# Two decoder layers on one core: later shift transposes, a wider order of the side work, a spread-out start, and GpSimd adding the two key halves of the exponentials

## What is computed

```python
x = layernorm(x + linear_attention(x))                     # "L0_attn", buckets of 64
x = layernorm(x + xattn(x, ctx))                           # two attentions, below
x = layernorm(x + moe(x, 16 experts, top 4, gelu))         # every expert on every token
x = layernorm(x + causal_attention(x, 16 heads of 64))
x = layernorm(x + cross_attention(x, ctx, 16 heads of 8))
x = layernorm(x + moe(x, 8 experts, top 2, capacity 40, relu))

def mha(x, y, ..., causal):                                # twice in xattn: on itself, then on ctx
    q, k, v = ln(x) @ wq, ln(y) @ wk, ln(y) @ wv           # 16 heads of 32
    a = softmax(q @ k.T * 32 ** -0.5)
    if causal: a = a * keep_earlier_keys                   # after the softmax: all keys stay in the sum
    x = x + a @ v @ li1 + b1
    return x + gelu(ln(x) @ li2 + b2) @ li3 + b3
```

## Time and profile before

| | |
|---|---|
| median of 3 runs (lowest to highest) | 918.81 us (918.29 to 922.25) |
| the profiled execution's own time | 918.41 us |
| its span, first to last instruction | 916.6 us |
| busy: PE, DVE, ACT, POOL | 776.5, 490.6, 433.4, 194.0 us |
| mean granted TensorE clock | 0.91 of full |

### The profile page before, as it was taken

One profiled execution on the slowest core, in us unless ns is written; L12 is line 12 of the kernel. 1 busy time (PEld: TensorE's weight loads), 2 busy tenths in 40 slices (PEclk: granted clock), 3 DMA queues, 4 the chain that ended last, 5 costly groups with the idle time before them and its releaser, 6 DMA issues.

```text
span 916.6 us, 16466 instructions
## 1 busy us (share of the span) xinstructions
PE 776.5 (85%) x6048; PEld 564.3 (62%) x6048; DVE 490.6 (54%) x1345; ACT 433.4 (47%) x1079; POOL 194.0 (21%) x272
## 2 busy tenths in 40 slices
PE   3675888887879798899999998989888888989866
PEld 1344666655655565568989896867665454757555
DVE  3675684746455565624454336544455666564542
ACT  1121556445454545474454447656553554434301
POOL 1111453434321211111000005432331010101100
PEclk9855998979798997999999999999999798989989
DMA  9206651514233443400000000000001400000000
GB/s 272 79 4 136 141 129 42 114 45 97 55 89 100 111 106 81 142 1 1 1 1 1 1 1 2 2 1 1 1 2 47 139 2 2 2 8 2 6 6 8
DMA packets 20496, 45.34 MB, mean 49 GB/s; under 512 B 5721, under 2 KB 9385, under 8 KB 20417
## 3 DMA queue, kind: packets, MB, share of 16 engines
q1 hardware_dynamic: 18688, 40.83, 17.6%
q10 hardware_dynamic: 1728, 3.45, 1.2%
HBM read 17.89 MB, written 0.52 MB: 20 GB/s over the span
## 4 chain that ended last, share of the span: by engine, by line
PE 67%; DVE 13%; ACT 9%; issue 7%; DMA 2%; SPq 2%; ACTq 0%; POOL 0%; POOLq 0%; DVEq 0%
PE G L502 10%; PE SC L681 7%; PE SC L743 6%; PE SC L730 6%; PE SM L692 5%; PE SO L715 5%; PE G L544 4%; PE G L507 3%; ACT causal_probs L1061 3%; PE SC L657 3%; PE G L842 2%; PE SO L797 2%; PE SC L765 2%; PE SM L664 2%; DVE negmax L1442 2%
## 5 line engine op out<-in xcount | busy, mean ns | idle before, releaser
L1076 ACT ACTIVATE exps<-SC 128x512 f32<-128x512 f32 x192 | 113.2, 599 | 144.4 <-PE SC L681 143.7
L1434 DVE TENSOR_REDUCE shift_cols<-SC 128x2 f32<-128x512 f32 x192 | 130.6, 687 | 62.0 <-PE SC L657 61.5
L1511 POOL TENSOR_TENSOR rstd<-variance,consts 128x2 f32<-128x2 f32 x52 | 37.0, 712 | 317.9 <-DVE variance L1136 317.9
L1577 POOL TENSOR_TENSOR unit_sums<-unit_sums,unit_inverse 128x256 f32<-128x256 f32 x48 | 35.5, 740 | 261.3 <-ACT unit_inverse L1082 261.3
L1050 ACT ACTIVATE hidden<-SC,cols 128x256 f32<-128x256 f32 x128 | 53.6, 471 | 68.5 <-PE SC L730 68.4
L1061 ACT ACTIVATE causal_probs<-SC,negmax 128x128 f32<-128x128 f32 (+1 forms) x128 | 52.3, 424 | 40.8 <-DVE negmax L1442 40.6
L681 PE MATMUL SC<-stacked_q,stacked_k 100*128 100x256 f32 x256 | 69.0, 355 | 1.7 <-DMA stacked_q<-shift_rows 0.8
L743 PEld LDWEIGHTS SC<-ffn_w,hidden 128*128 128x128 f32 x512 | 66.9, 194 | 5.3 <-issue 2.0
L1587 POOL TENSOR_TENSOR causal_probs<-causal_probs,inverse 128x256 f32<-128x256 f32 x64 | 51.6, 828 | 81.3 <-DVE inverse L1447 81.3
L1468 DVE SCALAR_TENSOR_TENSOR R<-SC,small,R 128x128 f32<-128x128 f32 x128 | 39.0, 346 | 55.4 <-PE SC L743 55.0
L743 PE MATMUL SC<-ffn_w,hidden 128*128 128x128 f32 x512 | 68.5, 278 | 0.0
(11 more groups left out here) (259 smaller groups left out, 1532.3 us busy)
## 6 DMA issues: line engine op xcount, KB each, us to landing
stacked_k<-k_hi SPq DMA_DIRECT2D x64, 128.0 KB, 2.4
stacked_q<-q_hi SPq DMA_DIRECT2D x64, 128.0 KB, 2.4
ffn_w<-in_ffn_w SPq DMA_DIRECT2D x16, 512.0 KB, 4.5
stacked_k<-k_lo SPq DMA_DIRECT2D x32, 128.0 KB, 2.4
stacked_q<-q_lo SPq DMA_DIRECT2D x32, 128.0 KB, 2.4
rows<-in_rows ACTq DMA_DIRECT2D x1, 840.0 KB, 6.5
a_weights<-in_a_li ACTq DMA_DIRECT2D x3, 256.0 KB, 8.7
w_a_li<-in_a_li SPq DMA_DIRECT2D x3, 256.0 KB, 4.6
```

The lines of the kernel that those rows point to most:

```text
L1076: fn(exps[:, n % EXPS, :, :].rearrange("p t q -> p (t q)"), SC[1][:, n % 2, :, :].rearrange("p t q -> p (t q)"), ACT.Exp, scale=ATTENTIONS ...
L1434: v.tensor_reduce(shift_cols[:, n // UNIT % 4, :, n % UNIT], SC[0][:, n % 2, :, :], axis=AX.X, op=ALU.max, negate=True).then_inc(head_max, 1)
```

## The change

1. TURN_AT goes from 5 to 6: PE's transposes, ACT's copy and SP's shift DMA of a unit come one slot later, three slots ahead of their use and no longer four.
2. The order of the sides: `project` starts at 16s-8 (before 16s-11) and draws its values at steps 14 and 15, which is slots 16s+6 and 16s+7; DVE copies both value tiles, where ACT copied one. `enter`, `route` and `causal_in` move by 1 to 3 slots. SP's stacks lie at steps 2, 4, 6, 9 and 12.
3. Slack: PE's transposes behind a norm, and what follows from them, come one or two slots later than DVE's normalising (in `after`: 4 to 5, 5 to 6, 11 to 13, 17 to 20, 14 to 17; in `mix` the 25 steps become 31; in `settle` and `causal_out` one more slot).
4. Start and loads: `linear` starts at slots -22, -13, -6 and 2; qkv is loaded first; the waits for constants, tables and masks move to where they are used; DVE converts the masks at slot 0; the weights of the later stages are loaded by SP in `after(0)` and not ahead of the first stacks.
5. In A2 and LX POOL adds the two key halves of each head's exponentials into `kept` (128x256), at the slot behind the exponential, and PE's `unit_sum` then takes 4 matmuls in place of 8 and waits for POOL.

```diff
-TURN_AT, SUMS_AT, INVERT_AT, VALUES_AT, REFINE_AT, DIVIDE_AT = 5, 15, 16, 17, 17, 18
+TURN_AT, SUMS_AT, INVERT_AT, VALUES_AT, REFINE_AT, DIVIDE_AT = 6, 15, 16, 17, 17, 18
...
-    return FIRST + (0, 2, 5, 8)[b]
+    return (FIRST, FIRST + 9, FIRST + 16, 2)[b]
...
-    return HEADS * b - 12
+    return HEADS * b - 10
...
-    return HEADS * s - 11
+    return HEADS * s - 8
...
                 def unit_sum(U_):
                     n = UNIT * U_
-                    pe.wait_ge(head_exp, n + UNIT)
                     g = fill(pe, "unit", ("S", U_))
-                    for kt in range(TT):
+                    if stream_of(n) // NB == A1:
+                        pe.wait_ge(head_exp, n + UNIT)
+                        for kt in range(TT):
+                            for k in range(UNIT):
+                                last = mm(g[HD * k:HD * k + HD, 0:T], ones, exps[:, (n + k) % EXPS, kt, :],
+                                          start=kt == 0, stop=kt == TT - 1)
+                    else:
+                        pe.wait_ge(kept_ready, n + UNIT)
                         for k in range(UNIT):
-                            last = mm(g[HD * k:HD * k + HD, 0:T], ones, exps[:, (n + k) % EXPS, kt, :],
-                                      start=kt == 0, stop=kt == TT - 1)
+                            last = mm(g[HD * k:HD * k + HD, 0:T], ones,
+                                      kept[(n + k) % EXPS].rearrange("p t q -> p (t q)"), start=True, stop=True)
...
-                    yield 24
-                    copied(("v", s, 0), values(s, 0, 0, 512), lambda g: g[:, :])
...
+                def add_key_tiles(n):
+                    pool.wait_ge(head_exp, n + 1)
+                    wait_filled(pool, ("O" if stream_of(n - EXPS) // NB == A1 else "S", (n - EXPS) // UNIT))
+                    if n == STACK_HEADS:
+                        wait_filled(pool, ("OC", 4 * NB - 1))
+                    v.tensor_tensor(kept[n % EXPS].rearrange("p t q -> p (t q)"), exps[:, n % EXPS, 0, :],
+                                    exps[:, n % EXPS, 1, :], ALU.add).then_inc(kept_ready, 1)
...
                     if n is not None and stream_of(n) // NB == A1:
                         keep(n)
+                    elif n is not None:
+                        add_key_tiles(n)
...
-                for group in ("ctx", "a2", "m0", "lx", "m1", "l1"):
+                for group in ("ctx", "a2"):
                     load_group(group)
...
-                    yield 3
+                    yield 2
                     stack(s, "k", U_)
                     yield 4
                     stack(s, "q", U_)
-                    for j, step in ((1, 7), (2, 10), (3, 13)):
+                    for j, step in ((1, 6), (2, 9), (3, 12)):
```

More of the change, by code:

```diff
@@ L142, in route_at @@
 def route_at(b):
-    return after_at(NB + b) + 16 if b < 2 else after_at(2 * NB - 1) + 17
+    return after_at(NB + b) + 19 if b < 2 else after_at(2 * NB - 1) + 20
 def settle_at(b):
@@ L150, in causal_in_at @@
 def causal_in_at(b):
-    return settle_at(b) + 4 if b < 2 else L1_AT + PAIRS * (b - 1) + 1
+    return settle_at(b) + 5 if b < 2 else L1_AT + PAIRS * (b - 1) + 1
 def causal_out_at(b):
@@ L1171, in heads, with make_masks, make_choice @@
                     return x.rearrange("p (h d) -> p h d", d=HD0)
-                dve.wait_ge(consts_in, 16)
-                at = CONSTS["ident"][0] + 3 * HD
-                v.tensor_copy(choice, consts[3 * HD:3 * HD + UNIT, at:at + UNIT].unsqueeze(2).to_broadcast([UNIT, UNIT, T]))\
-                    .then_inc(masks_made, 1)
-                dve.wait_ge(mask_parts_in, 16)
-                for k, part in enumerate((pair_of16, later_pair16, first_of16, second_of16)):
-                    v.tensor_copy(part[:, :], mask_parts[:, k * P:(k + 1) * P]).then_inc(masks_made, 1)
-                dve.wait_ge(tables_in, 32)
+                def make_masks():
+                    dve.wait_ge(mask_parts_in, 16)
+                    for k, part in enumerate((pair_of16, later_pair16, first_of16, second_of16)):
+                        v.tensor_copy(part[:, :], mask_parts[:, k * P:(k + 1) * P]).then_inc(masks_made, 1)
+                def make_choice():
+                    dve.wait_ge(consts_in, 16)
+                    at = CONSTS["ident"][0] + 3 * HD
+                    v.tensor_copy(choice, consts[3 * HD:3 * HD + UNIT, at:at + UNIT].unsqueeze(2)
+                                  .to_broadcast([UNIT, UNIT, T])).then_inc(choice_made, 1)
                 def linear(b):
@@ L1250, in project @@
                                 op0=ALU.mult, op1=ALU.subtract).then_inc(*emptied((side, s, m)))
-                    yield 25
-                    g = wait_filled(dve, ("v", s, 1))
-                    v.tensor_copy(values(s, 1, 0, 512), g[:, :]).then_inc(*emptied(("v", s, 1)))
+                    for t in range(TT):
+                        yield 14 + t
+                        g = wait_filled(dve, ("v", s, t))
+                        v.tensor_copy(values(s, t, 0, 512), g[:, :]).then_inc(*emptied(("v", s, t)))
                 def after(s):
@@ L1472, in front @@
                 def front(slot):
+                    if slot == 0:
+                        make_masks()
                     if head_of(slot) is not None:
@@ L1647, in after @@
                 def after(s):
+                    if s == 0:
+                        for group in ("m0", "lx", "m1", "l1"):
+                            load_group(group)
                     if s == NB - 1:
-                        yield 13
+                        yield 15
                         wait_filled(sp, ("li3", s, 1))
```

135 lines of the change are left out of this document (69 added, 66 removed).

## The result

| | before | after |
|---|---|---|
| median of 4 runs (lowest to highest) | 919.03 us (918.29 to 922.25) | 862.21 us (857.17 to 872.49) |
| profiled execution, its span | 918.41, 916.6 us | 867.06, 865.3 us |

The ratio is 0.934, with a 95% interval of 0.926 to 0.942. Ratios leave out executions that are over 1.5% above the fastest of their kernel (here 872.49 us), medians do not. The time forecast was 862.

The account below looks back on a forecast made before the run. PE's program order, with a few late producers in it, was taken to set the time. Attention -44 (-27 - 12 - 8 - 12 + 15), LX -13, start 0: 918.8 - 57 = 862 us; range 835 to 903.

Parts of the forecast that it names:

- Bank and gelu, -27: Attentions: later transposes and moved gelu cut PE's 30.4 us of waits for the shared bank to 3.5, -27 us.
- Slack, -12: Attentions: transposes placed later behind a norm remove 12 of PE's 15.0 us of norm waits.
- Clock, -12: Attentions: 25 of 61 us at 1.2 GHz return to full clock, -12 us; bounds 0 and -26.
- the clock doesn't rise: Rival: no clock gain in the attentions, 874 us; inside the forecast's range, whose chance of 0.60 includes it.
- What comes back, +15: Attentions: removed waits uncover others (score bank ring, ACT's latency, SP's queue), +15 us; bounds 0 and 45.
- 0, and 5 us once: SP's later weight loads beside stream 2's stacks: no cost, or 5 us once if the stacks lack spare slots.
- The rival of the shift row as the bound: Rival: PE waits for shift DMAs at 28 units, deciding from 2 us each; at 2.7 us each 937 us; chance 0.05.
- Adds, -16 and +4: POOL's adds halve unit sums, -8 us in A2 and -8 in LX; longer normalising through the port lock, +4 us.
- the second rival: POOL gives nothing: lock costs 16 us in place of 4, lighter sums lower the clock, 4 us; 878 us, chance 0.08.
- Start, 0: Before slot 16: first scores at 70 us, 8 earlier, but DVE work moves into slots 0 to 11; 0, bounds -10 and +10.
- slot 16 at 100 to 105 us: Last step of the start term: slot 16 reached at 100 to 105 us, against 101.5 before the change.
- LX and the end, -13: Third attention to the end: waits -9, sums -8, port +2, uncovered waits +2, together -13 us.

Follow-up runs that it names:

- e6: The kernel before with TURN_AT = 6 alone: 890.4 us, ratio 0.969.
- e7: The kernel before with the first feed-forward matmul (li2) and its gelu one slot later, no other edit: 902.6 us.
- e8: The kernel before with POOL's adds and the halved unit sums in A2 only: 919.1 us, ratio 1.000.
- e2: The kernel before with POOL's adds and the halved unit sums in both A2 and LX, no other edit: 935.8 us, ratio 1.014.
- e4: The changed kernel with the four linear attentions back at their old start slots (-22, -20, -17, -14): 850.8 us, ratio 0.921.
- e9: The changed kernel with the old start slots and POOL's adds in A2 only: 845.0 us, ratio 0.923.
- e1: The changed kernel without POOL's adds, unit sums of 8 matmuls again in A2 and LX: 875.0 us.
- e3: The changed kernel with TURN_AT back at 5, the gelu staying at its new slot: 861.2 us, ratio 0.932.
- e13: The changed kernel with old start slots, adds in A2 only, TURN_AT 5 in LX and SP's later weight loads seven slots later: 859.9 us, ratio 0.933.

## Why the prediction came out

The mechanism of the attentions was right; that the number came to within a microsecond is luck. The changed kernel's own runs are spread over 15 us, and in the profiles the parts add up to -51.3 us where -57 was forecast: the start cost 10.3 us where 0 was booked, the attentions gave 50.1 and not 44, the last stage 9.9 and not 13, and the middle 1.6 and not 0.

**Bank and gelu, -27: right, and for the reason given, but the shares weren't.** Of 30.0 us of waits for the logarithm none is left, where 3.5 us were kept. I wrote of the gelu's 3.3 us stalls, and these are only half of it, five waits. The other half are short waits, which the later turn removes and the moved gelu doesn't (e6, e7).

**Slack, -12: right.** The norm waits between the marks are 16.9 us before and 5.4 after.

**Clock, -12: right in the attentions and too small there, absent from the whole.** In the attentions the share at 1.2 GHz falls from 22% of 295.4 us to 10% of 245.3, so 40 us return and not 25, worth about 18 us (40 x 0.9 busy / 2). Together with the 8 us of sums that is 26, and the busy time fell by 23.8; the booked terms were 8 + 12. No term was booked for the clock elsewhere, and there the start and the last stage took nearly as much time at 1.2 GHz as the attentions gave back. The rival "the clock doesn't rise" is true of the whole span, and false of the stage that it was meant for.

**What comes back, +15: the size was right.** (Its upper bound of 45 was more than the 39 us that the two wait terms had booked.) The idle time falls by 26.3 us, where the three idle terms gave 27 + 12 - 15 = 24. The largest new wait is a kind that I named, the shift row behind SP's queue, and I had set SP's loads at "0, and 5 us once": it is 5.42 us, once. Timelines of SP (last load, last stack issue before the shift row, and the shift row) and of PE:

```profile
146.06 0.43 SPq L1630 DMA_DIRECT2D w_l_wo<-in_l_wo  x1
...
150.09 1.57 SPq L1654 DMA_DIRECT2D stacked_q<-q_lo  x1
151.70 0.71 SPq L1683 DMA_DIRECT2D stacked_q<-shift_rows  x1
```

```profile
156.16 0.80 PE L680 MATMUL SC<-stacked_q,stacked_k 100*128 100x256 f32 x2 [5.42 <-DMA stacked_q<-shift_rows]
```

The rival of the shift row as the bound fell: 8.4 us in 3 waits, where it needed 2 us at each of 28 units.

**Adds, -16 and +4: the sum holds for A2 in the changed kernel, the argument behind it doesn't.** GpSimd's add, and DVE's normalising in A2, cost what was read from A1:

```profile
L1591 POOL TENSOR_TENSOR VB<-exps x128: 715/727/1256, 236.2 to 810.4; 128x256 f32<-128x256 f32 x128
```

```profile
L1150 DVE TENSOR_SCALAR Z<-R,moments,rstd x8: 334/744/891, 253.5 to 349.1; 128x128 f32<-128x128 f32 x8
```

In LX, for which A1's price was booked too, most of the normalising is as short as without adds (the same line from 650 to 850 us):

```profile
L1150 DVE TENSOR_SCALAR X<-R,moments,rstd x10: 336/341/766, 668.1 to 826.5; 128x128 f32<-128x128 f32 x10
```

TensorE waits for GpSimd for 0.2 us in all. But I priced the adds as if half a microsecond of TensorE in a unit were half a microsecond anywhere. e8 shows that without slack A2's are worth nothing (the second rival's mechanism, in the kernel where nothing covers the longer normalising). e2 shows that in LX of the kernel before less work for TensorE went with a lower clock that cost more than it saved, 17 us net; the prediction had this as 4 us in a rival. In the changed kernel's order LX's adds show neither gain nor loss beyond the noise: e4 against e9 and e1's last stage say so, and e3, which has them, has the shortest last stage of all.

**Start, 0: wrong; it costs 10.3 us, the end of the bound.** The first scores came at 68.7 us (forecast 70), but the first values at 113.6. The step that failed is the last, "slot 16 at 100 to 105 us": I took DVE as nearly busy through slots 0 to 11. Slot 16 came at 112.7 us, behind the 110 us that the prediction named as a sign of being wrong. Windows after:

```profile
40.00:68.60 28.60, 17.48 (x57) 10.74 (x58) 15.70 (x63) 6.99 (x17) 2.83 (x4) 0.62 0.23 51
68.60:113.60 45.00, 31.80 (x130) 22.10 (x129) 31.64 (x96) 11.54 (x27) 9.10 (x14) 0.66 0.29 64
```

From the first scores to the first values DVE is busy for 31.6 of 45 us, 70%. Up to the first values its work is the same in both kernels, 63 us; four chains abreast fitted it into 103 us, one or two at a time need 114.

**LX and the end, -13: -9.9 in the profile.** Waits for the norm and for the router's choice, 16.4 us before, are no longer among the long ones. The two halves of the term are both off: TensorE's idle time fell by 14.6 us, where 9 less 4 was booked, and its busy time rose by 4.7 us, where the sums were to take 8 away, at a stage mean clock of 0.84 against 0.90. The unchanged middle stages moved by -4.2 and +2.6.

## To carry to other kernels

Before moving a step that waits, look in the waited engine's own order for what stands ahead of the producer: here two table loads and a gelu ahead of a 0.4 us copy cost five waits of 3.3 us, and taking them away also took 18.6 us of busy time by a higher clock (e7). And read the clock in every stage: here the time at 1.2 GHz that the attentions lost came back at the start and in the last stage. An edit that takes work from the bound engine is worth its time only if the order leaves room for what it costs the others, so test it with and without the slack. Spreading dependent chains to start the first one sooner can end later: count when the shared engine's whole work is done, not when the first consumer starts.

## What the runs showed of the hardware

TensorE can be busy for 10.00 of 10 us, window after window, and stay at 1.2 GHz: the three windows of e9 above. Of the 163 matmul records of these 30 us 48 are the third attention's scores, with 24 or 25 operand rows, and 92 the sums and values of a unit; with 32 rows in the scores, the added products zero, the time was the same (843.6 and 845.0 us). In the profiles, one execution of each kernel, the first such stretch of the last stage is 27 to 41 us long in the seven kernels with LX's turn at 6, 10 to 20 us in six with it at 5, and 38 us in a seventh (e13). What starts and ends them stays open.

Executions of one kernel differ with the clock: e4 took 846.0 and 847.2 us at mean clocks of 0.922 and 0.927, and 854.4 and 856.2 us at 0.905 and 0.907. It isn't so in all: e3's 855.1 and 863.9 us have 0.925 and 0.930. Removing sum matmuls of the last stage went with a lower clock in the kernel before (0.88 in e2 against 0.90 to 0.91 in e8); in the changed order that isn't shown.
